# Product-key stage: maxima subtracted as the bias of per-head exponentials, one list in PSUM, the next tile normalised by ScalarE

## Chip, core and metric

The kernel runs on one core of a Trainium2 chip. It computes a whole decoder of four layers in one launch. The metric is device time in microseconds, the median of three runs. The engines are TensorE (PE; PEld is its weight load), VectorE (DVE), ScalarE (ACT), GpSimd (POOL) and SyncE (SP), each with its own instruction queue; they are kept in order by semaphores.

## The reference, cut to the stage

The input is 8 x 128 x 256: eight tiles of 128 tokens with 256 features. Twelve blocks follow one another; the change lies in the ninth, the feed-forward of the third layer, a retrieval by product keys:

```python
x = x + _L2_ffn_ref(_layernorm(x, axis=-1), ...)

h = silu(x W_up + b_up) W_down + b_down          # 256 -> 1024 -> 128
q = (h W_q), 2 halves x 8 heads x 64
sim = einsum('pbthn,hkpn->pbthk', q, keys)       # 2 x 8 heads x 45 similarities
scores, idx = lax.top_k(sim, 8)
all_scores = scores[0][..., :, None] + scores[1][..., None, :]
sc, pk = lax.top_k(all_scores, 8)                # the best 8 of 64 pairs
z = einsum('btd,bthkd->bthk', h, down_embed[indices])
z = silu(z * softmax(sc))
out = einsum('bthk,bthkd->btd', z, up_embed[indices])
```

The kernel gathers nothing. For each head it forms all 45 x 45 = 2025 pair weights as the outer product of the exponentials of the two halves, masks those below the eighth best pair, and multiplies with z for all 2025 entries.

## The kernel before

The stage handles one tile of 128 tokens after the other, n = 0 to 7. A tile has 16 items g = 16n + s: eight heads for entries 0 to 1023 (s = 0 to 7), and eight heads for entries 1024 to 2024 (s = 8 to 15). The order of every engine is written out by hand in loops over n and s; the preparation of tile n+1, and the normalising of tile n+2, are placed between items of tile n.

For one item, GpSimd makes the outer product of 23 x 45 weights (`L2f_outer`, L1320) into a ring of seven buffers `P_r`, running up to five items ahead. VectorE compares it with the threshold and multiplies by z, the mask (`L2f_mask`, L3132). The product of mask and weights is taken by VectorE (`L2f_prod`, L3140), or by GpSimd for s = 2, 5, 10 and 13 (`L2f_poolprod`, L1328), into a ring of six buffers `Q_r`. ScalarE applies silu with the reciprocal of the sum as its scale (`L2f_silu`, L1988). TensorE transposes and sums over heads in PSUM (`L2f_acc`, L4347). After eight items ScalarE copies the sums out (`L2f_gt`, L1992 to L1997), and TensorE multiplies by the up embedding (`L2f_out`, L4356); VectorE adds the residual (`L2f_resid`, L3144). z itself is a product of TensorE in PSUM (`L2f_z`, L4337), one for each half of a tile; TensorE issues z of half 0 of tile n+1 at s = 15, behind the transposes of item 13 (`L2f_acc(g - 2)`), and the mask of s = 0 waits for it.

Preparation of tile n+1 on the way through tile n: up projection (L4158) at s = 0, its silu (`L2f_he`, L1862) at s = 2, down, query and similarity products (L4165, L4171, L4284) at s = 3 to 5 with the evictions L1946, L1950 and L1954 (`L2f_simc`) on ScalarE. All of these use `pro`, two PSUM banks. Then:

- `L2f_top` (VectorE, s = 7): 16 MAX8 instructions (L3096) into `top8`, and a subtraction of the maximum from the lists into `top8s` (L3099).
- `L2f_sub` (GpSimd, s = 7): the maximum is subtracted from all 720 similarities (L1307). It is queued ahead of the outer product of item 12.
- `L2f_exp` (ScalarE, s = 10, behind silu 9): a table load (L1957), the exponential of the lists (L1959), and that of the 720 similarities (L1961).
- `L2f_rstd` (ScalarE, s = 10, for tile n+2): a table load (L1847), Ln (L1849), Exp (L1851). The next silu loads its table again.
- `L2f_u` (VectorE, s = 13, for tile n+2): the normalised tile (L2981). TensorE transposes it at s = 14 (`L2f_uT`, L4149), behind the transposes of item 12, and ScalarE copies it at s = 15 (`L2f_unT`, L1857).
- `L2f_thresh` (VectorE, s = 15): the 64 candidate products of each head (L3104), the eighth best (L3107), the sum of the best eight (L3110) and its reciprocal (L3112).
- GpSimd's first outer product of tile n+1 is queued at s = 11 of tile n, behind the outer product of item 15, and waits for L1961. Its product of item 13 is queued two outer products later.

## Time and profile before

| | |
|---|---|
| median of 3 runs | 2097.64 us (2092.2 to 2108.24) |
| the profiled execution's own time | 2106.74 us |
| its span | 2105.0 us, mean granted TensorE clock 0.942 |
| busy over the span | PE 88%, PEld 65%, DVE 70%, ACT 51%, POOL 52% |
| outer product on GpSimd (L1320) | 128 x, mean 1969 ns |
| product on GpSimd (L1328) | 32 x, mean 2153 ns |
| product on VectorE (L3140), 1024 elements, one input in PSUM | 96 x, mean 1212 ns |
| Ln over one column with a pointer bias (L1849), Exp over one column (L1851) | mean 296 and 203 ns |
| GpSimd's subtraction (L1307) waiting for the maxima (L3096) | 9.3 us in 5 of 8 |

The profile is that of one execution. Busy times count an engine's instructions; idle time before an instruction is put down to the instruction whose semaphore came last. In the timeline, instructions of one line that follow one another are merged into one row with their count, so that a row's duration runs from the first start to the last end. Line numbers are those of the kernel before.

### The profile page before, as it was taken

The page shows a single profiled execution, that of the slowest core. Times are in us where ns is not written, and L with a number is a line of the kernel's source. Part 1 is how long each engine was busy: PE and PEld are TensorE (multiplying, and loading weights), DVE is VectorE, ACT ScalarE, POOL GpSimd, SP SyncE. Part 2 cuts the span into 40 slices and gives each one's busy share as a digit, 9 for nine tenths or more (in the row PEclk, how much of TensorE's full clock was granted, in tenths as well). Part 3 has the DMA queues.
Part 4 walks back from the last instruction along what each step waited for, and adds up shares of the span by engine and source line. Part 5 has one row for each costly group of instructions (what it writes and reads, how often), then busy time and mean ns, then how long its engine had stood idle before and what let it go on. Part 6 is the DMA issues. An engine that isn't in the chain of part 4 may idle for free.

```text
span 2105.0 us, 31292 instructions
## 1 busy us (share of the span) xinstructions
PE 1847.7 (88%) x11466; PEld 1373.4 (65%) x11466; DVE 1483.6 (70%) x2496; ACT 1071.2 (51%) x2328; POOL 1095.8 (52%) x800
## 2 busy tenths in 40 slices
PE   7767789799899987899999999968888789998999
PEld 5111148545789975677777777757777665567887
DVE  5788943465764576677777777589999978866554
ACT  4444421244322254666666666556667556655443
POOL 3699930121691064655555555499999940023321
PEclk9788989689899998999999999989999989999999
DMA  5211001040400000110000000000000001000000
GB/s 165 46 35 35 0 1 59 20 161 0 181 1 1 1 21 21 51 34 1 1 1 1 1 1 31 28 3 1 1 1 1 26 26 58 1 1 1 6 9 9
DMA packets 20544, 54.87 MB, mean 26 GB/s; under 512 B 8111, under 2 KB 11864, under 8 KB 17960
## 3 DMA queue, kind: packets, MB, share of 16 engines
q1 hardware_dynamic: 20392, 52.88, 7.5%
q8 instruction: 92, 1.51, 0.3%
q14 instruction: 60, 0.49, 0.1%
HBM read 44.48 MB, written 1.05 MB: 22 GB/s over the span
## 4 chain that ended last, share of the span: by engine, by line
PE 54%; DVE 19%; POOL 11%; issue 8%; ACT 7%; SPq 1%; DMA 0%; DVEq 0%; POOLq 0%; ACTq 0%
POOL sbuf L1320 5%; PE psum L4187 4%; DVE sbuf L2319 4%; PE psum L4250 3%; PE psum L3537 2%; POOL sbuf L1328 2%; PE psum L4347 1%; DVE psum L3132 1%; PE psum L4653 1%; PE psum L4219 1%; PE psum L4235 1%; PE psum L4191 1%; PE psum L4199 1%; PE psum L3516 1%; ACT sbuf L1902 1%
## 5 line engine op out<-in xcount | busy, mean ns | idle before, releaser
L1320 POOL TENSOR_TENSOR sbuf<-sbuf 128x1035 f32<-128x1035 f32 x128 | 248.3, 1969 | 0.9 <-ACT sbuf L1961 0.9
L4347 PE MATMUL psum<-sbuf 128*128 128x128 f32 (+1 forms) x1024 | 146.6, 294 | 57.3 <-ACT sbuf L1988 41.7
L1988 ACT ACTIVATE sbuf<-sbuf 128x1001 f32<-128x1001 f32 (+1 forms) x128 | 141.9, 1139 | 97.4 <-DVE sbuf L3140 64.6
L4347 PEld LDWEIGHTS psum<-sbuf 128*128 128x128 f32 (+1 forms) x1024 | 127.9, 154 | 78.1 <-ACT sbuf L1988 58.6
L1275 POOL TENSOR_TENSOR sbuf<-sbuf 128x512 f32<-128x512 f32 x64 | 66.7, 1042 | 187.7 <-DVE sbuf L3004 187.7
L1115 POOL TENSOR_TENSOR sbuf<-sbuf 128x1024 f32<-128x1024 f32 x64 | 150.0, 2355 | 17.2 <-DVE sbuf L2319 16.1
L2319 DVE TENSOR_TENSOR_SCAN sbuf<-psum,sbuf 128x1024 f32<-128x1024 f32 x64 | 144.6, 2277 | 14.4 <-POOL sbuf L1115 7.5
L1902 ACT ACTIVATE sbuf<-psum,sbuf 128x128 f32<-128x128 f32 x256 | 90.4, 365 | 107.2 <-DVE sbuf L2998 107.2
L3483 PE MATMUL psum<-sbuf 96*128 96x512 bf16 x256 | 82.8, 432 | 61.7 <-DVE sbuf L2319 35.4
L3132 DVE SCALAR_TENSOR_TENSOR psum<-sbuf,psum 128x1024 f32<-128x1024 f32 (+1 forms) x96 | 122.3, 1274 | 11.5 <-PE psum L4337 4.2
L1445 ACT ACTIVATE psum<-psum,sbuf 128x1016 f32<-128x1016 f32 x64 | 68.9, 1081 | 120.9 <-PE psum L3483 120.9
L4187 PE MATMUL psum<-sbuf 128*128 128x512 f32 x256 | 123.9, 607 | 3.5 <-POOL sbuf L1271 3.5
L3140 DVE TENSOR_TENSOR sbuf<-psum,sbuf 128x1024 f32<-128x1024 f32 (+1 forms) x96 | 116.4, 1212 | 3.3
L3483 PEld LDWEIGHTS psum<-sbuf 96*128 96x128 bf16 x256 | 18.5, 102 | 139.0 <-DVE sbuf L2319 67.1
L4250 PE MATMUL psum<-sbuf 128*128 128x256 bf16 x768 | 94.6, 273 | 14.4 <-POOL sbuf L1283 14.2
L1281 POOL TENSOR_TENSOR sbuf<-sbuf 128x512 f32<-128x512 bf16 x64 | 74.4, 1163 | 49.7 <-DVE sbuf L3017 48.0
L4250 PEld LDWEIGHTS psum<-sbuf 128*128 128x128 bf16 x768 | 71.3, 98 | 39.8 <-POOL sbuf L1283 30.7
L1373 POOL TENSOR_TENSOR sbuf<-sbuf 128x1024 f32<-128x1024 f32 x16 | 30.8, 1944 | 121.8 <-DVE sbuf L3333 121.8
L2993 DVE TENSOR_TENSOR sbuf<-psum,sbuf 128x512 f32<-128x512 f32 x64 | 44.3, 691 | 57.1 <-ACT sbuf L1886 57.1
L1283 POOL TENSOR_TENSOR sbuf<-sbuf 128x512 bf16<-128x512 f32 x64 | 81.1, 1268 | 5.0
L3516 PE MATMUL psum<-sbuf 128*32 128x512 f32 x256 | 78.9, 748 | 3.9 <-POOL sbuf L1115 3.8
L1328 POOL TENSOR_TENSOR sbuf<-sbuf 128x1024 f32<-128x1024 f32 (+1 forms) x32 | 68.9, 2153 | 18.3 <-DVE sbuf L3132 18.3
(811 smaller groups left out, 5093.2 us busy)
## 6 DMA issues: line engine op xcount, KB each, us to landing
sbuf<-sbuf SPq DMA_DIRECT2D x50, 128.0 KB, 2.4
sbuf<-w_p_d SPq DMA_DIRECT2D x8, 512.0 KB, 3.9
sbuf<-w_qkv_d SPq DMA_DIRECT2D x3, 768.0 KB, 4.2
sbuf<-w_e_d SPq DMA_DIRECT2D x1, 2048.0 KB, 8.0
sbuf<-w_gu_d SPq DMA_DIRECT2D x1, 2048.0 KB, 10.2
sbuf<-w_gu_d SPq DMA_DIRECT2D x2, 1024.0 KB, 8.0
sbuf<-w_dn_d SPq DMA_DIRECT2D x1, 2048.0 KB, 16.5
sbuf<-w_q_d SPq DMA_DIRECT2D x1, 2048.0 KB, 8.5
```

Source lines behind the costliest of these rows:

```text
L1115: pool.tensor_tensor(L0a_hc[i % 4][:, :], L0a_hs[i % 2][:, :], L0a_Cr[g % 4][:, :], ALU.mult).then_inc(hc_done, 1)
L1320: pool.tensor_tensor(P_r[g % 7][:, :, :], rows.unsqueeze(2).to_broadcast([128, 23, 45]), cols.unsqueeze(1).to_broadcast([128, 23, 45]), AL ...
L1328: pool.tensor_tensor(Q_r[g % 6][:, 0:w], M_r[L2f_pool_items(g) % 2][:, 0:w], Pf_r[g % 7][:, o:o + w], ALU.mult).then_inc(poolprod_done, 1)
L1902: last = act.activation(prob[:, h, :], L2x_s[:, h, :], ACT.Exp, bias=smax[:, h:h + 1], accum_out=esum[:, h:h + 1])
L1988: act.activation(Q_r[g % 6][:, 0:w], Q_r[g % 6][:, 0:w], ACT.Silu, scale=q8_p[n % 2][:, h:h + 1]).then_inc(silu_done, 1)
L2319: dve.tensor_tensor_scan(L0a_hs[i % 2][:, :], L0a_dAf[i % 2][:, :], L0a_us[i % 3][:, :], 0.0, ALU.mult, ALU.add).then_inc(scan_done, 1)
L3132: dve.scalar_tensor_tensor(M[:, 0:w], Pf_r[g % 7][:, o:o + w], t8_p[n % 2][:, h, 7:8], zps[:, 0:w], ALU.is_ge, ALU.mult).then_inc(mask_don ...
L3140: dve.tensor_tensor(Q_r[g % 6][:, 0:w], Mps[:, 0:w], Pf_r[g % 7][:, o:o + w], ALU.mult).then_inc(prod_done, 1)
L3483: last = pe.matmul(out[:, 512 * h:512 * h + 512], rows, L0a_stack[g % 4][0:96, a, 512 * h:512 * h + 512], start=True, stop=True)
L4187: last = pe.matmul(L2x_q[:, :, :], xs[:, vq, c, :], wq[:, c, 512 * g:512 * g + 512], start=c == 0, stop=c == 1)
L4250: last = pe.matmul(L2x_out[:, :], cat16[:, h, :], w_p3[p][:, 4 * (i % 8) + h, :], start=i % 8 == 0 and h == 0 and p == 0, stop=i % 8 == 7 ...
L4347: last = pe.matmul(Gps[0:m, c, :], Q_r[g % 6][:, 128 * c:128 * c + m], ident[:, :], start=h == 0 and c % 4 == 0, stop=h == 7, skip_group_c ...
```

## The change

The subtraction of the maxima goes from GpSimd and VectorE to ScalarE. The lists of the eight largest lie beside the similarities, in columns 45 to 52 of rows that are now 53 long. VectorE's second instruction in `L2f_top` only negates the 16 maxima. `L2f_exp` is 24 activations, each with the negated maximum of its head as a pointer bias: eight over 53 columns for the second half (similarities and list together), eight over 8 columns for the first half's list, written to PSUM (`top8e`, in a gap of `pro`), and eight over 45 columns. `L2f_u` for tiles 2 to 7 becomes `L2f_standard` on ScalarE, three activations that wait on one another, at s = 12, between silu 11 and silu 12. TensorE gets two waits, and its transposed tile moves to other columns of `pro`.

```diff
--- before.py
+++ after.py
@@ -568,18 +568,18 @@
         GT = view(sbuf, 35862, [16, 128])
         he = view(sbuf, 38934, [8, 128])
         qc = view(sbuf, 39958, [8, 128])
-        sim_p = [view(sbuf, 40982 + 720 * p, [2, 8, 45]) for p in range(2)]
-        top8 = view(sbuf, 42422, [2, 8, 8])
+        sim_p = [view(sbuf, 40982 + 848 * p, [2, 8, 53]) for p in range(2)]
+        top8n = view(sbuf, 42678, [2, 8])
         h2T_p = [view(sbuf, 46152 + 128 * p, [128]) for p in range(2)]
         cand = view(sbuf, 46408, [8, 8, 8])
         t8_p = [view(sbuf, 46920 + 64 * p, [8, 8]) for p in range(2)]
         q8_p = [view(sbuf, 47048 + 8 * p, [8]) for p in range(2)]
         d8 = view(sbuf, 47064, [8])
-        top8s = view(sbuf, 47072, [2, 8, 8])
         zps = view(psum, 3072, [1024])
         Mps = view(psum, 1024, [1024])
         Gps = view(psum, 2048, [8, 128])
         pro = view(psum, 0, [1024])
+        top8e = view(psum, 360, [8, 8])
 
         L2f_pool_heads = (2, 5)
 
@@ -697,17 +697,17 @@
                      'clip': 2, 'expo': 4, 'magic': 4, 'sum': 8, 'q': 1, 'k': 8, 'v': 12, 'sq': 12, 'ss': 4, 'lnvar': 13, 'rstd': 13, 'norm': 20,
                      'vc': 12, 'qTc': 9, 'kTc': 12, 'score': 12, 'max': 24, 'exp': 24, 'recip': 12, 'prob': 4, 'pT': 24, 'pTc': 24, 'o': 12,
                      'cat': 7, 'proj': 20, 'resid': 28, 'hi': 5, 'mid': 5, 'lo': 5}
-        L2f_start = {'stats': 46, 'ln': 16, 'factor': 15, 'u': 30, 'uT': 18, 'unT': 18, 'up': 12, 'down': 4, 'q': 65, 'score': 76, 'max': 88,
+        L2f_start = {'stats': 46, 'ln': 16, 'factor': 15, 'u': 30, 'centred': 13, 'prep': 11, 'uT': 18, 'unT': 18, 'up': 12, 'down': 4, 'q': 65, 'score': 76, 'max': 88,
                      'sub': 24, 'exp': 88, 'mask': 1, 'prod': 40, 'silu': 16, 'sum': 40, 'proj': 84, 'resid': 36}
         L3a_start = {'const': 9, 'bn': 46, 'stats': 62, 'u': 38, 'uT': 26, 'unT': 26, 'q': 73, 'v': 76, 'lnvar': 77, 'rstd': 77, 'norm': 84,
                      'vc': 76, 'qTc': 73, 'kTc': 76, 'score': 84, 'max': 96, 'exp': 96, 'recip': 76, 'pT': 88, 'pTc': 88, 'o': 76, 'cat': 71,
-                     'proj': 92, 'resid': 44, 'sub': 32, 'aoT': 4, 'bias': 4}
-        L3x_start = {'context': 1, 'clip': 34, 'expo': 36, 'k': 72, 'vc': 84, 'summary': 1, 'spread': 8, 'gate': 12, 'oclip': 64, 'prep': 11,
+                     'proj': 92, 'resid': 44, 'sub': 24, 'aoT': 4, 'bias': 4}
+        L3x_start = {'context': 1, 'clip': 34, 'expo': 36, 'k': 72, 'vc': 84, 'summary': 1, 'spread': 8, 'gate': 12, 'oclip': 64, 'prep': 17,
                      'oexpo': 64, 'exp': 128, 'qT': 64, 'ln': 24, 'osum': 64, 'oq': 16, 'ratio': 36, 'sum': 168, 'factor': 23, 'norm': 100,
                      'proj': 100, 'resid': 52}
         L3f_start = {'const': 10, 'bn': 54, 'stats': 70, 'u': 46, 'uT': 34, 'unT': 34, 'q': 81, 'v': 84, 'ss': 68, 'lnvar': 85, 'rstd': 85, 'vc': 92,
                      'qTc': 81, 'kTc': 84, 'score': 116, 'mask': 129, 'max': 128, 'exp': 136, 'recip': 92, 'prob': 68, 'pT': 120, 'pTc': 120,
-                     'o': 92, 'cat': 79, 'proj': 108, 'resid': 60, 'sub': 64, 'ur': 8, 'xr': 16, 'mod': 4, 'low': 4, 't': 4, 'gate': 20, 'up': 20,
+                     'o': 92, 'cat': 79, 'proj': 108, 'resid': 60, 'sub': 56, 'ur': 8, 'xr': 16, 'mod': 4, 'low': 4, 't': 4, 'gate': 20, 'up': 20,
                      'silu': 144, 'prod': 136}
         L0a_later_loaded = stack.enter_context(nc.semaphore('L0a_later_loaded'))
         L0a_stack_loaded = [stack.enter_context(nc.semaphore(f'L0a_stack{s}_loaded')) for s in range(4)]
@@ -1301,11 +1301,6 @@
 
             pool.wait_ge(resid_done, L2x_start['resid'] + 8)
 
-            def L2f_sub(n):
-                pool.wait_ge(simc_done, n + 1)
-                pool.wait_ge(max_done, L2f_start['max'] + n + 1)
-                pool.tensor_tensor(sim_p[n % 2][:, :, :, :], sim_p[n % 2][:, :, :, :], top8[:, :, :, 0:1].to_broadcast([128, 2, 8, 45]), ALU.subtract).then_inc(sub_done, 1)
-
             def L2f_outer(g):
                 n, half, h = g // 16, g // 8 % 2, g % 8
                 if g % 16 == 0:
@@ -1316,7 +1311,7 @@
                     else:
                         pool.wait_ge(prod_done, L2f_start['prod'] + L2f_dve_items(g - 6))
                 rows = sim_p[n % 2][:, 0, h, 22 * half:22 * half + 23]
-                cols = sim_p[n % 2][:, 1, h, :]
+                cols = sim_p[n % 2][:, 1, h, 0:45]
                 pool.tensor_tensor(P_r[g % 7][:, :, :], rows.unsqueeze(2).to_broadcast([128, 23, 45]), cols.unsqueeze(1).to_broadcast([128, 23, 45]), ALU.mult).then_inc(outer_done, 1)
 
             def L2f_poolprod(g):
@@ -1327,14 +1322,11 @@
                     pool.wait_ge(sum_done, L2f_start['sum'] + g - 5)
                 pool.tensor_tensor(Q_r[g % 6][:, 0:w], M_r[L2f_pool_items(g) % 2][:, 0:w], Pf_r[g % 7][:, o:o + w], ALU.mult).then_inc(poolprod_done, 1)
 
-            L2f_sub(0)
             for g in range(5):
                 L2f_outer(g)
             for n in range(8):
                 for s in range(16):
                     g = 16 * n + s
-                    if s == 7 and n < 7:
-                        L2f_sub(n + 1)
                     if L2f_by_pool(g):
                         L2f_poolprod(g)
                     if g + 5 < 128:
@@ -1850,11 +1842,21 @@
                 act.wait_ge(ln_done, L2f_start['ln'] + n + 1)
                 act.activation(st0[:, 9:10], st0[:, 8:9], ACT.Exp, scale=-0.5).then_inc(factor_done, 1)
 
+            def L2f_standard(n):
+                act.wait_ge(stats_done, L2f_start['stats'] + 2 * n + 2)
+                act.activation(st0[:, 10:11], st0[:, 6:7], ACT.Copy, scale=-1.0).then_inc(prep_done, 1)
+                act.wait_ge(uT_done, L2f_start['uT'] + n)
+                act.wait_ge(prep_done, L2f_start['prep'] + n - 1)
+                act.activation(u0[:, :], x[:, n, :], ACT.Identity, bias=st0[:, 10:11]).then_inc(centred_done, 1)
+                act.wait_ge(centred_done, L2f_start['centred'] + n - 1)
+                act.wait_ge(factor_done, L2f_start['factor'] + n + 1)
+                act.activation(u0[:, :], u0[:, :], ACT.Copy, scale=st0[:, 9:10]).then_inc(u_done, 1)
+
             def L2f_unT(n):
                 act.wait_ge(uT_done, L2f_start['uT'] + n + 1)
                 if n == 0:
                     act.wait_ge(ratio_done, L2x_start['ratio'] + 32)
-                act.activation(unT0[:, 0:2, :], L2x_uT[:, :, :] if n == 0 else pro[:, 0:256].rearrange('p (c s) -> p c s', c=2), ACT.Copy).then_inc(unT_done, 1)
+                act.activation(unT0[:, 0:2, :], L2x_uT[:, :, :] if n == 0 else pro[:, 768:1024].rearrange('p (c s) -> p c s', c=2), ACT.Copy).then_inc(unT_done, 1)
 
             def L2f_he(n, a, b):
                 act.wait_ge(up_done, L2f_start['up'] + n + 1)
@@ -1951,14 +1953,19 @@
 
             def L2f_simc(n):
                 act.wait_ge(score_done, L2f_start['score'] + n + 1)
-                act.activation(sim_p[n % 2][:, :, :, :], pro.rearrange('p (q c) -> p q c', q=2)[:, :, 0:360].rearrange('p q (h k) -> p q h k', h=8), ACT.Copy).then_inc(simc_done, 1)
+                act.activation(sim_p[n % 2][:, :, :, 0:45], pro.rearrange('p (q c) -> p q c', q=2)[:, :, 0:360].rearrange('p q (h k) -> p q h k', h=8), ACT.Copy).then_inc(simc_done, 1)
 
             def L2f_exp(n):
                 act.preload_act_table_set('natural_log_exp_and_others')
                 act.wait_ge(shift_done, n + 1)
-                act.activation(top8s[:, :, :, :], top8s[:, :, :, :], ACT.Exp).then_inc(exp_done, 1)
-                act.wait_ge(sub_done, L2f_start['sub'] + n + 1)
-                act.activation(sim_p[n % 2][:, :, :, :], sim_p[n % 2][:, :, :, :], ACT.Exp).then_inc(simexp_done, 1)
+                for h in range(8):
+                    act.activation(sim_p[n % 2][:, 1, h, :], sim_p[n % 2][:, 1, h, :], ACT.Exp, bias=top8n[:, 1, h:h + 1])
+                for h in range(8):
+                    last = act.activation(top8e[:, h, :], sim_p[n % 2][:, 0, h, 45:53], ACT.Exp, bias=top8n[:, 0, h:h + 1])
+                last.then_inc(exp_done, 1)
+                for h in range(8):
+                    last = act.activation(sim_p[n % 2][:, 0, h, 0:45], sim_p[n % 2][:, 0, h, 0:45], ACT.Exp, bias=top8n[:, 0, h:h + 1])
+                last.then_inc(simexp_done, 1)
 
             def L3a_rstd(n):
                 act.wait_ge(stats_done, L3a_start['stats'] + n + 1)
@@ -2031,6 +2038,8 @@
                             L2f_exp(n + 1)
                             if n < 6:
                                 L2f_rstd(n + 2)
+                        if s == 12 and n < 6:
+                            L2f_standard(n + 2)
                         if s == 15 and n < 6:
                             L2f_unT(n + 2)
             L2f_silu(127)
@@ -3090,18 +3099,18 @@
                 dve.wait_ge(simc_done, n + 1)
                 if n > 0:
                     dve.wait_ge(cand_done, n)
-                    dve.wait_ge(sub_done, L2f_start['sub'] + n)
+                    dve.wait_ge(simexp_done, n)
                 for p in range(2):
                     for h in range(8):
-                        last = dve.max(top8[:, p, h, :], sim_p[n % 2][:, p, h, :])
+                        last = dve.max(sim_p[n % 2][:, p, h, 45:53], sim_p[n % 2][:, p, h, 0:45])
                 last.then_inc(max_done, 1)
                 dve.wait_ge(max_done, L2f_start['max'] + n + 1)
-                dve.tensor_tensor(top8s[:, :, :, :], top8[:, :, :, :], top8[:, :, :, 0:1].to_broadcast([128, 2, 8, 8]), ALU.subtract).then_inc(shift_done, 1)
+                dve.tensor_scalar(top8n[:, :, :], sim_p[n % 2][:, :, :, 45], -1.0, None, ALU.mult).then_inc(shift_done, 1)
 
             def L2f_thresh(n):
                 t8, q8 = t8_p[n % 2], q8_p[n % 2]
                 dve.wait_ge(exp_done, L2f_start['exp'] + n + 1)
-                dve.tensor_tensor(cand[:, :, :, :], top8s[:, 0, :, :].unsqueeze(3).to_broadcast([128, 8, 8, 8]), top8s[:, 1, :, :].unsqueeze(2).to_broadcast([128, 8, 8, 8]), ALU.mult).then_inc(cand_done, 1)
+                dve.tensor_tensor(cand[:, :, :, :], top8e[:, :, :].unsqueeze(3).to_broadcast([128, 8, 8, 8]), sim_p[n % 2][:, 1, :, 45:53].unsqueeze(2).to_broadcast([128, 8, 8, 8]), ALU.mult).then_inc(cand_done, 1)
                 dve.wait_ge(cand_done, n + 1)
                 for h in range(8):
                     last = dve.max(t8[:, h, :], cand[:, h, :, :])
@@ -3172,8 +3181,6 @@
                             L2f_stats(n + 2)
                         if s == 7:
                             L2f_top(n + 1)
-                        if s == 13 and n < 6:
-                            L2f_u(n + 2)
                         if s == 15:
                             L2f_thresh(n + 1)
             L3a_values(0)
@@ -4145,12 +4152,16 @@
 
             def L2f_uT(n):
                 pe.wait_ge(u_done, L2f_start['u'] + n + 1)
+                if n > 2:
+                    pe.wait_ge(resid_done, L2f_start['resid'] + n - 2)
                 for k in range(2):
-                    last = pe.transpose(L2x_uT[:, k, :] if n == 0 else pro[:, 128 * k:128 * k + 128], u0[:, 128 * k:128 * k + 128], ident[:, :])
+                    last = pe.transpose(L2x_uT[:, k, :] if n == 0 else pro[:, 768 + 128 * k:896 + 128 * k], u0[:, 128 * k:128 * k + 128], ident[:, :])
                 last.then_inc(uT_done, 1)
 
             def L2f_up(n, a, b):
                 pe.wait_ge(unT_done, L2f_start['unT'] + n + 1)
+                if n > 0:
+                    pe.wait_ge(cand_done, n)
                 if n > 2:
                     pe.wait_ge(resid_done, L2f_start['resid'] + n - 2)
                 for j in range(a, b):
```

## Rows read from the trace of the kernel before

**Rows 1.** Busy us (instructions) of PE, PEld, DVE, ACT, POOL in one tile; clock, DMA, GB/s

```profile
1459.00:1502.00 43.00, 37.25 (x255) 32.38 (x254) 41.10 (x62) 29.87 (x42) 42.18 (x22) 0.95 0.00 1
```

**Rows 2.** Timeline, end of tile 2: start us, us, engine, line, tiles, count [idle before <-releaser]

```profile
1490.95 1.28 ACT L1957 ACT_TABLE_LOAD   x1
...
1492.24 0.31 ACT L1959 ACTIVATE sbuf<-sbuf 128x128 f32<-128x128 f32 x1
...
1492.46 0.79 ACT L1961 ACTIVATE sbuf<-sbuf 128x720 f32<-128x720 f32 x1
...
1493.27 1.28 ACT L1847 ACT_TABLE_LOAD   x1
...
1496.40 3.17 ACT L1988 ACTIVATE sbuf<-sbuf 128x1001 f32<-128x1001 f32 x3
...
1497.59 4.29 PE L4347 MATMUL psum<-sbuf 128*128 128x128 f32 x24 [2.60 <-ACT sbuf L1988]
...
1501.72 0.38 PE L4149 MATMUL psum<-sbuf 128*128 128x128 f32 x2
...
1502.81 1.89 PE L4337 MATMUL psum<-sbuf 128*128 128x512 f32 x4
...
1504.82 1.29 DVE L3132 SCALAR_TENSOR_TENSOR psum<-sbuf,psum 128x1024 f32<-128x1024 f32 x1 [0.20 <-POOL sbuf L1320]
```

**Rows 3.** Waits of the stage: engine, line, releaser: us in total, times, longest us

```profile
DVE psum L3132 <- PE psum L4337: 4.2, 4, 2.8
```

**Rows 4.** Source lines of four operations: duration ns min/median/max, first to last start, forms

```profile
L2981 DVE TENSOR_SCALAR sbuf<-sbuf x8: 402/500/1827, 1297.7 to 1624.2; 128x256 f32<-128x256 f32 x8
...
L3104 DVE TENSOR_TENSOR sbuf<-sbuf x8: 1240/1522/1880, 1368.1 to 1672.2; 128x512 f32<-128x512 f32 x8
...
L1320 POOL TENSOR_TENSOR sbuf<-sbuf x128: 1916/1951/2386, 1369.9 to 1708.2; 128x1035 f32<-128x1035 f32 x128
...
L4337 PE MATMUL psum<-sbuf x64: 571/592/1062, 1364.5 to 1699.0; 128*128 128x512 f32 x48, 128*128 128x489 f32 x16
```

**Rows 5.** Timeline of ACT, two pairs of activations with a pointer operand

```profile
436.92 0.51 ACT L1605 ACTIVATE sbuf<-sbuf 128x256 f32<-128x256 f32 x1 [5.50 <-DVE sbuf L2567]
437.33 0.49 ACT L1606 ACTIVATE sbuf<-sbuf 128x256 f32<-128x256 f32 x1
...
564.12 0.28 ACT L1714 ACTIVATE sbuf<-sbuf 128x1 f32<-128x1 f32 x1
564.31 0.28 ACT L1715 ACTIVATE sbuf<-sbuf 128x1 f32<-128x1 f32 x1
```

**Rows 6.** Timeline, tiles 0, 5 and 6: table load ahead of exponentials, mask 0 behind it

```profile
1404.84 1.28 ACT L1957 ACT_TABLE_LOAD   x1
...
1420.74 1.29 DVE L3132 SCALAR_TENSOR_TENSOR psum<-sbuf,psum 128x1024 f32<-128x1024 f32 x1 [0.20 <-POOL sbuf L1320]
...
1618.77 1.28 ACT L1957 ACT_TABLE_LOAD   x1
...
1633.86 1.29 DVE L3132 SCALAR_TENSOR_TENSOR psum<-sbuf,psum 128x1024 f32<-128x1024 f32 x1 [0.20 <-POOL sbuf L1320]
...
1661.73 1.28 ACT L1957 ACT_TABLE_LOAD   x1
...
1675.88 1.29 DVE L3132 SCALAR_TENSOR_TENSOR psum<-sbuf,psum 128x1024 f32<-128x1024 f32 x1 [0.20 <-POOL sbuf L1320]
```

**Rows 7.** Timeline, start of the stage

```profile
1367.80 0.31 ACT L1959 ACTIVATE sbuf<-sbuf 128x128 f32<-128x128 f32 x1 [1.00 <-DVE sbuf L3099]
...
1369.94 13.37 POOL L1320 TENSOR_TENSOR sbuf<-sbuf 128x1035 f32<-128x1035 f32 x7 [0.91 <-ACT sbuf L1961]
```

**Rows 8.** Timeline, tile 0: GpSimd and VectorE around the normalising pass

```profile
1406.85 5.73 POOL L1320 TENSOR_TENSOR sbuf<-sbuf 128x1035 f32<-128x1035 f32 x3
...
1410.91 1.83 DVE L2981 TENSOR_SCALAR sbuf<-sbuf 128x256 f32<-128x256 f32 x1
```

**Rows 9.** Busy us and granted clock just after TensorE restarts, tile 2

```profile
1499.00:1500.00 1.00, 1.00 (x7) 1.00 (x6) 0.90 (x2) 0.57 (x1) 1.00 (x1) 0.50 0.00 0
```


## The prediction

> **What bounds the kernel now.** The change touches one stage, 1365 to 1720 us. I read first the busy times by window: in a whole tile (43 us) VectorE is busy for 41.10 us and GpSimd for 42.18, TensorE for 37.25 and ScalarE for 29.87 [rows 1]. So the first reading is that VectorE and GpSimd share the bound and ScalarE has a third of its time free. Busy time does not say when that free time lies, so I read next the timeline around the end of one tile, item 9 of tile n to item 0 of tile n+1 [rows 2]. ScalarE there loads the table set at 1490.95, runs its two exponentials (1492.24 to 1493.27), loads twice more around the rstd pair, and runs silu 10 to 12 from 1496.40 to 1499.57. TensorE, idle for 2.60 us waiting for silu 10, then does transposes 10 to 12, the transpose of the next normalised tile (1501.72), transposes 13, and only then the matmuls of z for the next tile (1502.81, 1.89 long, so until 1504.70). VectorE's mask 0 of the next tile waits for z and starts at 1504.82. The two are 0.12 us apart: in this stretch the chain ScalarE, TensorE, z has next to no slack. The waits confirm it: mask was already held by z four times, 4.2 us in total, 2.8 at most [rows 3]. Whatever is put on ScalarE between silu 9 and silu 13 therefore comes out as VectorE time. This is where the sum is made.
>
> **What leaves VectorE and GpSimd.** GpSimd loses its subtraction (1.45 us, eight times). VectorE loses the normalising pass for six tiles, median 0.50 us but up to 1.83 [rows 4], and its candidate product, 1.52 us at the median for 512 elements with both inputs in SBUF, gets one input from PSUM; the stage's own product does 1024 elements with one input in PSUM in 1.2 us (table of the profile), so 512 take at most that and at least half of it; I take 0.7, saving 0.8. That is about 1.7 us of VectorE and 1.45 of GpSimd per tile. If these engines kept the bound, 42.5 us a tile would become about 41, or 10 to 12 us over the stage. I cost all this at nothing, because VectorE spends it waiting for z: both removed items lie behind item 9.
>
> **What comes onto ScalarE: the exponentials.** 24 activations replace two. Durations overlap, so starts must be used. With a per-partition pointer operand, two activations of one column start 0.19 us apart, two of 256 columns 0.41 apart [rows 5]; this is 0.187 + 0.00087 per column. 53, 8 and 45 columns then take 0.23, 0.19 and 0.23: 8 x 0.65 = 5.2 us, against 1.03 now (1492.24 to 1493.27). Lower end: without the pointer 128 columns take 0.22 from start to start [rows 2], 0.11 + 0.00087 per column, so 8 x 0.42 = 3.4 us. Upper end: no overlap at all, 24 x 0.30 (the Ln over one column, table) = 7.2. I take 5.2, since the rows with a pointer are the same form. Added: 4.2 us.
>
> **The normalising pass.** It comes behind silu 11 and ahead of silu 12: a copy of one column (0.20, as the rstd's Exp in the table), an Identity over 256 columns with a pointer (0.51), a scaled copy (0.49, both [rows 5]), each waiting on the one before, so without overlap: 1.2 us (0.9 to 1.5). No table load comes with it: the Identity and Copy evictions between silus have none today.
>
> **Sum for one tile.** Silu 12 ends at 1499.57 + 4.17 + 1.2 = 1504.9. Transposes 12 start 0.1 later, the normalised tile's transpose 0.87 after that (1505.9), z ends 2.98 behind it (1501.72 to 1504.70 in the rows) and mask 0 starts at 1509.0, that is 18.05 us after the table load. Now the six tiles that also normalise take 15.9, 14.5, 13.9, 15.3, 14.2 and 15.1 from that load to mask 0 (88.9 in all; [rows 6] has the first and the last of the six). 6 x 18.05 - 88.9 = 19.4 us. The work from mask 0 to the next load, 28 us (the five periods from 1420.74 to 1633.86 are 42.6 each, less the mean of 14.6 from load to mask), hangs on the same z and does not shrink: of what the change removes nothing lies there but GpSimd's subtraction, and GpSimd stands behind VectorE's mask 2 there.
>
> **Tile 6** has no normalising pass and no rstd, but GpSimd's first outer product of tile 7 waits for the last exponential, and its product 13 is queued behind it. From the load: 1.29 + 5.2 + 0.1, two outer products at 1.95 [rows 4], product 13 at 2.15 (table; 12.7), silu 13 (1.07), transposes and z (3.0): 16.8 against 14.15 now [rows 6]: 2.6 us. In the other six tiles product 13 is ready at 12.7 too, 1.3 ahead of where silu 13 can start.
>
> **The start.** The exponentials of tile 0 have no other work beside them. Now the small exponential starts at 1367.80 and GpSimd's first outer product at 1369.94 [rows 7]; then 1367.80 + 5.2 + 0.1 = 1373.1. 3.2 us, kept because tile 0 runs behind GpSimd's first seven outer products.
>
> **The lock.** The two-input subtraction over the lists becomes a tensor_scalar over 16 elements. The trace: the removed normalising pass is also a tensor_scalar in SBUF, and it needs 0.40 us alone but 1.83 when it starts at 1410.91 in a run of outer products that ends at 1412.58, and it ends just behind them [rows 4, 8]. So the new 16-element instruction can wait up to 1.95 us for the outer product in flight; today GpSimd mostly is between two instructions there, waiting for the maxima (9.3 us in five of the eight, table). Bounds: nothing, or 1.8 in each of seven tiles (12.6). By where GpSimd's outer products end today against VectorE's list subtraction, four of seven tiles would be caught (1.3 to 1.8 us), three not. Most of it is free: in tiles 1 to 5 the chain enters ScalarE through silu 9, which starts 1 us after its product is there, behind two copies of sums that hang on TensorE. I estimate that 0.7, 0.7, 0.2 and 0.2 remain, 1.8 us.
> The Trainium skill says it as a rule (SBUF - State Buffer, Who interferes with whom): a VectorE instruction in a two-port mode and a GpSimd instruction exclude each other for the whole instruction. By that rule, the trace agrees, 1.43 of the 1.83 us are a wait, and it is the new instruction that would meet it in every tile: rival D.
>
> **The clock.** TensorE's idle time ahead of transposes 10 grows from 2.6 to 6.8 us. After the present gap the granted clock was 0.50 (1.2 GHz) [rows 9], and the 24 matmuls took 4.29 us. The new transposes 12 start 3.2 us behind the restart (1501.8 to 1505.0), and today the transpose behind them, 4.1 us after the restart, runs at full speed (0.38 for two). I take 0.3 us a tile, 1.8; bounds 0 and (transposes 12, 13 and z, 4 us, at half clock) 24.
>
> **New waits of no cost.** Up-projection behind the candidate product: TensorE comes to it behind z, the product ends 4 us before. The transpose behind an earlier residual: that was added at item 12 of a tile, the transpose stands at item 14. The maxima behind the previous exponentials: those ended a tile ago.
>
> **Sum.** 19.4 + 2.6 + 3.2 + 1.8 + 1.8 = 28.8, so 29 us. The profiled execution took 2106.74 us (span 2105.0) and would become 2136; it lies 9 us over the median of the three runs, 2097.64, which becomes 2127 (+1.4%). Measurement of this kernel tells about 1% from no change.
>
> **Rivals.**
> A: ScalarE is not what holds mask 0 (not slower). Place: the 24 exponentials and the pass, between silu 9 and silu 12. They would have to cost together less than 3.1 us (14.8 average now - 11.65 for the rest of the chain) for VectorE and GpSimd to keep the bound; then their 1.45 to 1.7 us a tile count. For: ScalarE is 70% busy and both others over 95%. Against: even the lower end, 3.4 + 0.9, is above it. Price: 2097.6 - 11 = 2087. Chance 0.07.
> B: exponentials overlap more than the pointer rows say (3.4 us). 8 x 1.8 less: 2127 - 14 = 2113, within 1%. For: nothing depends on the one in front. Against: rows 5. Chance 0.12.
> C: the clock stays low until z is done. z alone costs 1.9 more in six tiles, 11 us: 2138. For: the longest z matmul of the trace is 1.06 us against 0.59 [rows 4]. Against: the clock had come back by transposes 12. Chance 0.12.
> D: the lock is hit in every tile and is not hidden, 1.8 x 7 instead of 1.8: 2138. Chance 0.09.
> E: the normalising pass does not run where it stands (a table load comes with it, 1.28 in six tiles): 2135. Chance 0.03.
> My forecast: 0.57.
>
> **Range and chances.** 2111 to 2142 takes in B, C, D and E and leaves out A and the far ends of the clock. Slower by over 1% (above 2118.6): forecast, C, D, E, 0.81. Within 1%: B and half of A, 0.15. Faster by over 1%: 0.04, since even A's full price is 0.5%.
>
> **What would show it.** From the table load of L2f_exp to mask 0 of the next tile about 18 us in tiles 0 to 5; mask waiting for z (TensorE) in each, 2.5 to 5 us, some 25 in all; the 24 exponentials 5.2 us from first to last start; GpSimd's busy share down from 97% to under 90% in the stage, with idle time released by ScalarE; the new tensor_scalar between 0.1 and 2 us in two clusters; a tile of 46 us instead of 42.5. Wrong would be: mask 0 released by the reciprocal as today; exponentials under 0.15 us apart; or a mask 0 that starts with z done long before, in which case rival A holds.

## The result, and the profile after

The changed kernel takes 2140.57 us (median of 4; 2126.8 to 2150.1) against 2096.6 beside it, ratio 1.0181 [1.0146, 1.0216]. The forecast was 2127, range 2111 to 2142, slower. The profiled execution took 2140.63 us, span 2138.7, 33.7 us more than before. The stages ahead of this one ended 6.9 us earlier in it (first MAX8 at 1358.69, before 1365.63; both stand at the same place in the code), so the stage itself gave away about 40 us. Those 6.9 us are not put down to the change: in the kernels below, which do not touch those stages, the first MAX8 starts anywhere from 1351.8 to 1367.7. The stage is therefore compared from trace to trace by its own length, from the first to the last mask 0: 304.0 us before, 340.4 after.

Lines moved: the table load L1957 is L1959, the exponentials are L1962, L1964 and L1967, the pass L1847, L1850 and L1853, MAX8 L3105, the negation L3108, mask L3141, product on VectorE L3149, candidates L3113, silu L1995, transposes and sums L4358, z L4348, outer product L1315. In some of the experiments they differ again by a few lines.

One whole tile by busy time (columns as in [rows 1]), the page's groups of mask and outer product, and the waits of VectorE in the stage:

```profile
1472.15:1520.16 48.01, 37.45 (x253) 33.05 (x251) 40.90 (x60) 34.43 (x65) 39.56 (x21) 0.89 0.00 1
```
```profile
L1315 POOL TENSOR_TENSOR sbuf<-sbuf 128x1035 f32<-128x1035 f32 x128 | 245.1, 1947 | 32.4 <-ACT sbuf L1967 32.4
...
L3141 DVE SCALAR_TENSOR_TENSOR psum<-sbuf,psum 128x1024 f32<-128x1024 f32 (+1 forms) x96 | 122.2, 1273 | 48.9 <-PE psum L4348 42.4
```
```profile
DVE psum L3141 <- PE psum L4348: 42.4, 9, 6.7
DVE sbuf L3105 <- ACT sbuf L1956: 7.0, 4, 5.6
```

Tiles 1 to 5 take 47.6 to 48.0 us instead of 42.0 to 43.5 (47.7 and 42.6 on average). GpSimd, 98% busy before, is busy for 39.56 of 48.01; ScalarE went from 29.87 to 34.43 and is still the least busy of the four. The mask's wait for z, 4.2 us in [rows 3], is 42.4. The chain behind it is seen in the timeline of the end of tile 2, the counterpart of [rows 2]:

```profile
1500.93 1.28 ACT L1959 ACT_TABLE_LOAD   x1
1502.23 1.95 ACT L1962 ACTIVATE sbuf<-sbuf 128x53 f32<-128x53 f32 x8
...
1504.08 1.59 ACT L1964 ACTIVATE psum<-sbuf 128x8 f32<-128x8 f32 x8
...
1505.61 1.88 ACT L1967 ACTIVATE sbuf<-sbuf 128x45 f32<-128x45 f32 x8
...
1507.51 1.28 ACT L1839 ACT_TABLE_LOAD   x1
...
1510.64 2.15 ACT L1995 ACTIVATE sbuf<-sbuf 128x1001 f32<-128x1001 f32 x2
...
1511.83 5.38 PE L4358 MATMUL psum<-sbuf 128*128 128x128 f32 x24 [7.41 <-ACT sbuf L1995]
1512.35 0.68 DVE L3113 TENSOR_TENSOR sbuf<-psum,sbuf 128x512 f32<-128x512 f32 x1
1512.70 0.18 ACT L1847 ACTIVATE sbuf<-sbuf 128x1 f32<-128x1 f32 x1
1512.98 0.51 ACT L1850 ACTIVATE sbuf<-sbuf 128x256 f32<-128x256 f32 x1
...
1513.52 0.51 ACT L1853 ACTIVATE sbuf<-sbuf 128x256 f32<-128x256 f32 x1
1513.94 3.16 ACT L1995 ACTIVATE sbuf<-sbuf 128x1001 f32<-128x1001 f32 x3
...
1517.01 0.47 PE L4158 MATMUL psum<-sbuf 128*128 128x128 f32 x2
...
1518.18 1.88 PE L4348 MATMUL psum<-sbuf 128*128 128x512 f32 x4
...
1520.16 1.29 DVE L3141 SCALAR_TENSOR_TENSOR psum<-sbuf,psum 128x1024 f32<-128x1024 f32 x1 [5.49 <-PE psum L4348]
```

From table load to mask 0 it is 19.23 us, 13.87 before. Split it where TensorE restarts: load to restart 10.90 (before 6.64), restart to the transposed tile 5.18 (before 4.13), from there to mask 0 3.15 (before 3.10). The first part grew by the exponentials. The second part grew because the clock is low for longer: granted clock by the microsecond, from the same tile:

```profile
1507.00:1508.00 1.00, 0.00 (x0) 0.00 (x0) 1.00 (x2) 0.98 (x4) 0.43 (x1) 0.50 0.00 0
...
1512.00:1513.00 1.00, 1.00 (x6) 1.00 (x7) 1.00 (x2) 0.91 (x3) 1.00 (x1) 0.50 0.06 16
...
1516.00:1517.00 1.00, 1.00 (x6) 1.00 (x5) 0.00 (x0) 1.00 (x2) 1.00 (x1) 0.50 0.00 0
1517.00:1518.00 1.00, 1.00 (x10) 1.00 (x10) 0.00 (x0) 0.58 (x3) 1.00 (x2) 0.92 0.00 0
```

and from the kernel before, behind its restart at 1497.59:

```profile
1500.00:1501.00 1.00, 1.00 (x8) 1.00 (x8) 0.97 (x2) 0.46 (x1) 1.00 (x2) 0.70 0.00 0
1501.00:1502.00 1.00, 1.00 (x12) 1.00 (x10) 1.00 (x2) 1.00 (x2) 1.00 (x1) 1.00 0.00 0
```

TensorE stood still for 7.41 us, was granted half of its 2.4 GHz from 1506.9 on, 4.9 us ahead of its restart, and got the rest back at 1517.2, 5.3 us behind it. Before, the clock fell at 1497.2, 0.4 us ahead of the restart, and was back at 1500.6, 3.0 us behind it. The 24 transposes took 5.38 us, before 4.29 [rows 2]; in a kernel below, at full clock, 8 take 1.04 to 1.10. In each of tiles 1 to 5 of the changed kernel the clock is low for 10.2 us; in the kernel before there are five low stretches of 3.4 us in these five tiles, and none in tile 3.

The lock, in the timeline of tile 0 (counterpart of [rows 8]) and as a source line:

```profile
1389.41 9.56 POOL L1315 TENSOR_TENSOR sbuf<-sbuf 128x1035 f32<-128x1035 f32 x5
...
1392.01 1.81 DVE L3105 MAX8 sbuf<-sbuf 128x8 f32<-128x45 f32 x16 [5.58 <-ACT sbuf L1956]
1393.85 5.14 DVE L3108 TENSOR_SCALAR sbuf<-sbuf 128x16 f32<-128x16 f32 x1
```
```profile
L3108 DVE TENSOR_SCALAR sbuf<-sbuf x8: 175/1744/5143, 1360.5 to 1683.4; 128x16 f32<-128x16 f32 x8
```

Sixteen elements take 0.175 us alone (tile 0's own maxima, at 1360.5) and 5.14 us when five outer products follow one another on GpSimd. The instruction began during the third of the five, which ended at 1395.1, and ended behind the fifth (1398.97). In five of the other six tiles it took 1.7 to 2.0 us: three times it ended with the outer product that was running when it began, twice with the next one, and each time another outer product followed at once. In the sixth it took 0.18. What decides how many go first was not tested.

### The profile page after: what moved, and what is told of

It is laid out like the page before. It is cut to its first block, busy times and chain, and to the rows that moved or that the text cites. A ratio compares the mean times of both kernels' runs of the same rounds, so it can differ in the third digit from the quotient of the medians.

```text
span 2138.7 us, 31477 instructions
## 1 busy us (share of the span) xinstructions
PE 1849.9 (86%) x11466; PEld 1382.7 (65%) x11466; DVE 1483.8 (69%) x2490; ACT 1112.6 (52%) x2522; POOL 1081.9 (51%) x792
## 3 DMA queue, kind: packets, MB, share of 16 engines
HBM read 44.48 MB, written 1.05 MB: 21 GB/s over the span
## 4 chain that ended last, share of the span: by engine, by line
PE 56%; DVE 18%; ACT 11%; POOL 7%; issue 7%; SPq 1%; DMA 0%; DVEq 0%; POOLq 0%; ACTq 0%
PE psum L4198 4%; PE psum L4358 3%; DVE sbuf L2328 3%; PE psum L4261 3%; PE psum L3544 2%; PE psum L4664 1%; PE psum L4230 1%; PE psum L4246 1%; POOL sbuf L1115 1%; PE psum L4202 1%; PE psum L4418 1%; ACT sbuf L1995 1%; POOL sbuf L1315 1%; PE psum L4210 1%; ACT sbuf L1904 1%
## 5 line engine op out<-in xcount | busy, mean ns | idle before, releaser
L1315 POOL TENSOR_TENSOR sbuf<-sbuf 128x1035 f32<-128x1035 f32 x128 | 245.1, 1947 | 32.4 <-ACT sbuf L1967 32.4
L4358 PE MATMUL psum<-sbuf 128*128 128x128 f32 (+1 forms) x1024 | 155.2, 308 | 85.4 <-ACT sbuf L1995 66.3
L4358 PEld LDWEIGHTS psum<-sbuf 128*128 128x128 f32 (+1 forms) x1024 | 138.5, 163 | 104.0 <-ACT sbuf L1995 83.6
L1995 ACT ACTIVATE sbuf<-sbuf 128x1001 f32<-128x1001 f32 (+1 forms) x128 | 141.9, 1141 | 94.1 <-DVE sbuf L3149 71.4
L3141 DVE SCALAR_TENSOR_TENSOR psum<-sbuf,psum 128x1024 f32<-128x1024 f32 (+1 forms) x96 | 122.2, 1273 | 48.9 <-PE psum L4348 42.4
L3149 DVE TENSOR_TENSOR sbuf<-psum,sbuf 128x1024 f32<-128x1024 f32 (+1 forms) x96 | 116.4, 1212 | 3.3
```

What stands on the lines that cost most here:

```text
L1315: pool.tensor_tensor(P_r[g % 7][:, :, :], rows.unsqueeze(2).to_broadcast([128, 23, 45]), cols.unsqueeze(1).to_broadcast([128, 23, 45]), AL ...
L1995: act.activation(Q_r[g % 6][:, 0:w], Q_r[g % 6][:, 0:w], ACT.Silu, scale=q8_p[n % 2][:, h:h + 1]).then_inc(silu_done, 1)
L3141: dve.scalar_tensor_tensor(M[:, 0:w], Pf_r[g % 7][:, o:o + w], t8_p[n % 2][:, h, 7:8], zps[:, 0:w], ALU.is_ge, ALU.mult).then_inc(mask_don ...
L3149: dve.tensor_tensor(Q_r[g % 6][:, 0:w], Mps[:, 0:w], Pf_r[g % 7][:, o:o + w], ALU.mult).then_inc(prod_done, 1)
L4358: last = pe.matmul(Gps[0:m, c, :], Q_r[g % 6][:, 128 * c:128 * c + m], ident[:, :], start=h == 0 and c % 4 == 0, stop=h == 7, skip_group_c ...
```

## The experiments

Two theories ran against each other. The first is the prediction's: ScalarE's longer queue makes z late, and z makes mask 0 late. The second came up on the way: the delay sits ahead of everything that TensorE does at a tile's end, the preparation of the next tile included, so that z's place does not matter. A smaller question was what the lock costs.

**The pass back on VectorE** (changed kernel otherwise).

```diff
...
-                        if s == 12 and n < 6:
-                            L2f_standard(n + 2)      # ScalarE
...
+                        if s == 13 and n < 6:
+                            L2f_u(n + 2)             # VectorE
```


> The changed kernel with the normalising pass back on VectorE (item 13). Theory (what ScalarE runs between silu 9 and silu 13 comes out one for one behind z): the pass's 1.2 us leave six tiles, so the table load to mask 0 of the next tile falls from 19.4 to about 18.2 us, or to 17.8 if TensorE's transposes 12 and 13 no longer have a transpose between them; 7 to 9 us under the changed kernel, about 35 over the one before. Rival (the exponentials alone hurt because of the lock at the new tensor_scalar): also about 35 over before, but then the distance from load to mask 0 stays at 19.4.

2142.97 us, ratio 1.0187 [1.0153, 1.0222]: nothing gained. The distance from load to mask 0 stayed at 19.2 to 19.5 us. That is what the rival expected, but for another reason: the kernel without the lock, below, keeps 19.35 to 19.5 us in tiles 3 to 5. The timeline of tile 2 in this kernel shows why the pass bought nothing.

```profile
1516.29 0.20 ACT L1843 ACTIVATE sbuf<-sbuf 128x1 f32<-128x1 f32 x1
...
1516.53 2.18 DVE L2978 TENSOR_SCALAR sbuf<-sbuf 128x256 f32<-128x256 f32 x1 [1.95 <-ACT sbuf L1843]
1517.81 5.21 ACT L1985 ACTIVATE sbuf<-sbuf 128x1001 f32<-128x1001 f32 x5
...
1518.99 5.38 PE L4348 MATMUL psum<-sbuf 128*128 128x128 f32 x24 [7.40 <-ACT sbuf L1985]
...
1527.33 1.29 DVE L3129 SCALAR_TENSOR_TENSOR psum<-sbuf,psum 128x1024 f32<-128x1024 f32 x1 [1.37 <-PE psum L4338]
```

Silu 10 to 14 now run without a gap, and the transposes still take 5.38 us, and mask 0 comes 8.34 us after the restart, as with the pass (8.33). So the pass's 1.2 us on ScalarE lay beside transposes that the low clock had stretched. VectorE in its turn stands 1.95 us for the reciprocal root, which waits behind the exponentials, and then takes 2.18 for a pass of 0.40 (the lock).

**The pass alone** (kernel before, with the pass on ScalarE).

```diff
...
+                        if s == 12 and n < 6:
+                            L2f_standard(n + 2)      # ScalarE
...
-                        if s == 13 and n < 6:
-                            L2f_u(n + 2)             # VectorE
```


> The kernel before with the normalising pass alone moved to ScalarE, item 12; exponentials, lists and subtraction as before. Theory: the chain silu 11, pass, silu 12, silu 13, z grows by 1.2 us in six tiles with next to no slack, minus nothing: 5 to 8 us over the kernel before, z releasing mask 0. Rival (VectorE holds mask 0, the chain has slack): VectorE loses 0.4 to 1.8 us a tile, so 3 to 6 us faster than before.

2099.62, ratio 0.999 [0.997, 1.001]. 1.2 us more on ScalarE, for 0.4 to 1.8 less on VectorE, cost nothing here: the 5 to 8 us of loss that the theory expected are outside the interval. The rival's gain of 3 to 6 us is inside it, and in the two traces the stage is 3.3 us shorter (300.7 for 304.0), 1.75 of it in tile 0. With the run above: the pass is not in the loss; the rest of the change, the 24 exponentials with the lists and the negation, carries it. What the negation adds by the lock is priced below.

**z early** (changed kernel).

```diff
                     g = 16 * n + s
+                    if s == 12 and n < 7:
+                        L2f_z(n + 1, 0)
                     if g >= 2:
                         L2f_acc(g - 2)
...
-                        if s == 15:
-                            L2f_z(n + 1, 0)
```


> The changed kernel, with TensorE's z of the next tile (half 0) put ahead of transposes 10 in its queue instead of behind transposes 13; nothing else. Theory (mask 0 is late only because z stands behind work that waits for ScalarE): mask 0 is released by the threshold instead, about 5 us earlier in tiles 0 to 5; about 1 us of each comes back because the up projection is no longer done earlier relative to mask 0; 20 to 30 us under the changed kernel. Rival (ScalarE's added work or GpSimd's wait for the exponentials is itself the bound of a tile): within 8 us of the changed kernel.

2139.73, ratio 1.0178 [1.0149, 1.0207]. The expectation was wrong, and partly through a slip: z writes the PSUM that mask 15 of the tile still reads. Waits of TensorE and VectorE in this kernel:

```profile
PE psum L4348 <- DVE psum L3141: 49.4, 7, 8.0
...
DVE sbuf L3105 <- ACT sbuf L1956: 28.0, 7, 5.8
...
DVE psum L3141 <- PE psum L4348: 4.1, 8, 2.1
```

The mask waits no more (4.1 us), but TensorE stands for mask 15 instead (49.4), and the MAX8 group waits for the similarities (28.0, in the changed kernel 7.0). So this run alone does not separate the theories. On the kernel before, the same edit was tried as well:

> The kernel before, with z of the next tile ahead of transposes 10 in TensorE's queue. The mask's 4.2 us of waiting for z would go, and TensorE would use 1.9 of its 2.6 idle us for z. If z is on the path of the kernel before (my reading of its timeline): 0.5 to 1 us per tile, 4 to 7 us in all, ratio 0.997. If VectorE and GpSimd bound it (41.1 and 42.2 us busy of 43): no change, ratio 1.000.

2134.96, ratio 1.0139 [1.011, 1.0167]: 29 us lost by moving the two matmul calls of z forward, where a small gain or none was expected. The timeline of a tile's end in it:

```profile
1504.05 1.04 PE L4347 MATMUL psum<-sbuf 128*128 128x128 f32 x8
1512.17 3.78 PE L4337 MATMUL psum<-sbuf 128*128 128x512 f32 x4 [7.08 <-DVE psum L3132]
```

z, at the lower clock (0.50 until 1517.6), takes 3.78 us, twice its 1.89 in [rows 2], and the transposes are queued behind it. No added ScalarE work is in this kernel, and tiles 1 to 5 take 47.7 us on average all the same (mask 0 from 1420.73 to 1659.25). So a pause of some 7 us of TensorE at a tile's end can come from another wait and give a tile as long.

**z in the middle** (changed kernel), the same test without that wait: in front of transposes 12, where mask 15 is long done.

```diff
+                    if s == 14 and n < 7:
+                        L2f_z(n + 1, 0)
                     if g >= 2:
                         L2f_acc(g - 2)
...
-                        if s == 15:
-                            L2f_z(n + 1, 0)
```


> The changed kernel with z of the next tile one group of transposes and the next tile's transposes ahead of its place: in front of transposes 12 instead of behind transposes 13. There mask 15, whose PSUM z overwrites, has ended long ago (in the changed kernel mask 15 ends at 1511.2 and transposes 12 start at about 1516.2), so z waits for nothing, unlike in the kernels with z in front of transposes 10, in which TensorE stood 7 us per tile in front of z. If the late z is what the added ScalarE work costs: mask 0 some 2.5 to 3 us earlier in seven tiles, 18 to 20 us, ratio 1.009. If the preparation of the next tile through TensorE (transposes, up projection, copy of the similarities, maxima, exponentials), which hangs on the same queue and does not move, closes the same loop: the MAX8 group waits for the similarities instead, 0 to 1 us per tile, ratio 1.015 to 1.018.

2145.61, ratio 1.0211 [1.0183, 1.0239]. Tiles 47.6 to 47.8 us, as in the changed kernel. Its timeline and waits:

```profile
1520.08 3.68 PE L4358 MATMUL psum<-sbuf 128*128 128x128 f32 x16 [6.86 <-ACT sbuf L1995]
1523.55 3.06 PE L4348 MATMUL psum<-sbuf 128*128 128x512 f32 x4
...
1526.70 1.29 DVE L3141 SCALAR_TENSOR_TENSOR psum<-sbuf,psum 128x1024 f32<-128x1024 f32 x1 [4.78 <-PE psum L4348]
```
```profile
DVE sbuf L3105 <- ACT sbuf L1956: 17.3, 7, 5.4
```

Mask 0 comes 6.6 us after the restart instead of 8.3, so the edit did what it says; the tile kept its length, and the MAX8 group waits 17.3 us instead of 7.0. In tiles 1 to 5 that wait is 1.9 us each, and it is what mask 0 had gained: from the load to mask 0 it is 17.4 to 17.6 us instead of 19.2 to 19.5, from mask 0 to the next load 30.2 instead of 28.2 to 28.8. That is the second theory: the preparation (transposes, up projection, similarities, maxima, exponentials) closes a loop over the same late restart, as long as the loop over z. "Mask 0 is held by z" is true and not the whole bound.

**No lock** (changed kernel).

```diff
-                dve.tensor_scalar(top8n[:, :, :], sim_p[n % 2][:, :, :, 45], -1.0, None, ALU.mult).then_inc(shift_done, 1)
+                dve.tensor_reduce(top8n[:, :, :], sim_p[n % 2][:, :, :, 45:46], AX.X, ALU.max, negate=True).then_inc(shift_done, 1)
```


> The changed kernel, with the negated maxima made by a negating tensor_reduce instead of a tensor_scalar (same 16 values). Theory (the tensor_scalar waits for the shared port): its row falls from 1.7 to 5.1 us to about 0.2 in all tiles. Tile 0 gains 4 us, the others 0.5 each since silu 9 had slack: 5 to 8 us under the changed kernel. Rival (the long rows are the instruction itself): its duration stays or the time doesn't move.

2132.65, ratio 1.0159 [1.0129, 1.0189], and all eight take 0.18 us:

```profile
L3108 DVE TENSOR_REDUCE sbuf<-sbuf x8: 181/182/185, 1357.3 to 1673.2; 128x16 f32<-128x16 f32 x8
```

From the first to the last mask 0 of the stage it is 333.2 us instead of 340.4. Of these 7.2 us, 5.6 are tile 0 (50.8 for 56.4); the other six share 1.6. The intervals of the two ratios overlap, so the price of the lock rests on this comparison of two traces.

**Both, z early and no lock.**

> The changed kernel with both edits of before at once: z of the next tile ahead of transposes 10 in TensorE's queue, and the maxima negated by a tensor_reduce instead of a tensor_scalar. With z early alone the tile kept its 47.8 us: the wait for z (5 us) went, and in its place stood 3.6 us of the MAX8 group waiting for the copy of the similarities and 3.4 to 4.9 us of the tensor_scalar behind outer products. Theory 1 (the two waits in its place are one behind the other, and the lock is the larger, since GpSimd runs five outer products without a pause there): without the lock 3 us in each of seven tiles go, tile 44.7 us, in all 20 us under z early alone and 12 under no lock alone: ratio to the kernel before about 1.008. Theory 2 (the tile is a loop through ScalarE, exponentials, silus, transposes, up projection, copy of the similarities, maxima, exponentials, and every wait off it only fills what is free): the lock lies in that loop too, but VectorE then waits for silu's buffers and the transposes instead; no more than tile 0's 5 us: ratio 1.015.

2125.23, ratio 1.0103 [1.0079, 1.0126], tiles 45.0 to 46.3, between the two expectations: with z early the MAX8 group is late, and a lock of 3.7 us (median with z early alone) behind it does stand on the path. Without the second table load as well:

> As z_early_no_lock, and the table load ahead of the rstd pair inside the loop is left out (the set is already there, loaded 6.5 us earlier for the exponentials): 1.28 us less on ScalarE between silu 9 and silu 10, in six tiles. Theory 2 (ScalarE's queue sets the tile): 1.28 x 6 = 7.7 us less than z_early_no_lock, ratio lower by 0.0037. Theory 1 (VectorE and GpSimd have the bound again once both waits are gone): no difference between the two.

2122.86, ratio 1.0082 [1.0053, 1.0111], and the same tiles to 0.1 us. The load taken out bought nothing there: TensorE stood for mask 15 at a tile's end (40.0 us in both), not for ScalarE. The kernel before with z early and one load gave 1.0139 [1.0113, 1.0164], again nothing on top of z early, and neither of its two expectations was met:

> The kernel before, z early as in before_z_early, and without the second load of the same table set ahead of the rstd pair inside the loop, 1.28 us of ScalarE in six tiles. If ScalarE between silu 9 and silu 12 is on the path: up to 7 us less than before_z_early, ratio 0.993 to 0.995. If VectorE and GpSimd bound the kernel before: no change, ratio 1.000 for both.

**One load** (changed kernel), the cleanest measure of what a microsecond of ScalarE's queue is worth. The second load of the same table set, ahead of the rstd pair, is left out inside the loop.

```diff
-                if n > 1:
-                    act.preload_act_table_set('natural_log_exp_and_others')
```


> The changed kernel without the second load of the same table set, ahead of the rstd pair inside the loop: 1.28 us less on ScalarE between silu 9 and silu 10, in six tiles, and nothing else. If ScalarE's queue behind silu 9 sets the tile, each us on it is a us of the tile: 7.7 us less than the changed kernel, ratio to the kernel before 1.0145, tiles 1 to 5 at 46.4 us instead of 47.7. Rival (the tile follows GpSimd and VectorE, and ScalarE's time is only seen in it): ratio 1.018, unchanged.

2125.76, ratio 1.0126 [1.0094, 1.0159]. The stage is 12.6 us shorter in the trace (327.8 for 340.4), where 7.7 were expected. Tiles 1 to 5 average 45.7 us (from 1419.09 to 1647.73) against 47.7: 2.0 us for 1.28. The pauses and transposes of tiles 1 and 2 in it:

```profile
1456.78 4.37 PE L4356 MATMUL psum<-sbuf 128*128 128x128 f32 x24 [5.44 <-ACT sbuf L1993]
...
1502.47 5.24 PE L4356 MATMUL psum<-sbuf 128*128 128x128 f32 x24 [5.99 <-ACT sbuf L1993]
```

Behind the shorter pause (5.44) the transposes take 4.37 us, and that tile is 45.1 long; behind 5.99 they take 5.24, and it is 46.4. In these two the clock came back earlier in the shorter tile (2.9 us behind the restart against 5.0), and the transposes account for 0.9 of the 1.3 us between them. The length of the pause alone does not decide it: in tile 0 of this kernel 24 transposes took 4.63 us behind 7.47, and in tile 0 of the last kernel below 5.36 behind 3.30.

**Three edits together** (changed kernel, z in the middle, no lock, one load).

> The three edits together on the changed kernel: z in front of transposes 12, the maxima negated by a tensor_reduce, one table load instead of two. If each works on the path by itself: 18 + 5 + 7.7 = 31 us less than the changed kernel, ratio 1.003 to 1.005. If the loop through the preparation binds: 7.7 + 5 + a part of 2 us per tile as in z_early_no_lock, about 15 to 25 us, ratio 1.006 to 1.011.

2124.42, ratio 1.0106 [1.0073, 1.0139]. From first to last mask 0 it is 321.5 us against 327.8 with one load alone: the difference is tile 0 and the lock, z's place adds nothing. The second expectation, by the loop through the preparation, held.

**The pass on ScalarE, one load** (kernel before), the try at a faster one.

> The kernel before with the normalising pass of the next tile on ScalarE (1.2 us there, 0.4 to 1.8 us less on VectorE), which alone changed nothing (0.999), and the second table load of the rstd pair left out (1.28 us less on ScalarE, same place). ScalarE's queue behind silu 9 is then as long as in the kernel before, and VectorE has 0.4 us less, 1.8 in tile 0. If ScalarE's queue and VectorE bound the tile together: 1.28 of z's lateness goes, 0.4 to 1.2 us per tile, 3 to 7 us, ratio 0.996 to 0.998, faster than both kernels. If GpSimd (42.2 of 43 us) is the bound: 0.999 as with the pass alone.

2094.92, ratio 0.9987 [0.9962, 1.0011]: no difference that can be told. Its tile 2:

```profile
1451.29:1493.35 42.06, 35.63 (x253) 30.48 (x251) 40.17 (x60) 28.71 (x42) 41.23 (x22) 1.00 0.00 1
```

The granted clock is 1.00 over the whole tile (0.96 before, over the tile from mask 0 to mask 0), the transposes run at full speed (8 in 1.04 to 1.10 us), and tiles 1 to 6 average 42.3 us against 42.5. They average 42.3 with the pass alone too, so the 1.28 us taken off ScalarE's queue between these two kernels gave nothing. GpSimd is busy for 41.23 of 42.06. This fits a kernel before in which GpSimd and VectorE bound the tile about as closely as the chain does: 1.2 us added to the chain or 1.28 taken off it change nothing, 4.2 cost all of it and the clock. The load left out of the kernel before by itself was not run.

## Why the prediction was right, and where it was off

Right in sign and near in size. 2140.6 against 2127 is 13.5 us, 1.4 us inside the upper end of the range, and the four executions lie between 2126.8 and 2150.1, so some luck is in that. The loss was forecast at 28.8 us; the ratio makes it 38, the traces 39.6 in the stage. The mechanism held (ScalarE's queue delays TensorE's restart, and z then holds mask 0). Two terms were mis-sized: the clock, and the lock. Step by step:

- *The exponentials.* 5.2 us forecast, 5.26 measured (1502.23 to 1507.49); the restart of TensorE came 4.26 us later from the load, against 4.2 added. The spacing from the pointer rows [rows 5] held for 53, 8 and 45 columns, into PSUM too. Rival B falls.
- *The pass.* 1.2 us on ScalarE, as forecast, but not on the path: taking it off the changed kernel gave nothing, and putting it on the kernel before cost nothing. So "whatever is put on ScalarE between silu 9 and silu 13 comes out as VectorE time" was wrong for it. This did not spoil the sum, by luck: in [rows 2] silu 12 ends at 1499.57 and transposes 12 begin at about 1500.85, a slack of 1.3 us that the pass just fills. The exponentials alone give the same figure, 13.87 + 4.17 = 18.04 us. Rival E falls, no load came with it.
- *The clock.* Here the sum was too small: 0.3 us a tile, where 1.0 to 1.3 were needed. The transposes 10 to 12 lasted 5.38 us, and the next tile's transposes ended up 16.1 us after the load where 14.95 was forecast. The argument had been that the clock, seen at full speed 4.1 us behind the restart before (it was back after 3.0), would be back for transposes 12. Behind a pause of 7.4 instead of 2.6 us it came back 5.3 us behind the restart, and transposes 12, from 1515.3 to the transposed tile at 1517.0, ran at half of it. Rival C had the mechanism half right: the transposes paid, z did not (1.88 us).
- *Load to mask 0.* 18.35 with the clock term, measured 19.2 to 19.5 in tiles 0 to 5 (116.4 in sum against 88.9): 27.5 us, forecast 21.2. Tile 6: 16.88, forecast 16.8; there product 13 ended 12.75 us behind the load, forecast 12.7. Start: from MAX8 to mask 0 3.1 us more, forecast 3.2.
- *The lock.* The term "four of seven caught, 1.8 us remain" was mis-sized: 7.2 us by the kernel without it. Six of seven were caught. Its upper bound for one wait, one outer product in flight, failed in tile 0: it lasted over the rest of three, 5.14 us. Rival D (a lock in every tile, 1.8 each) had the count nearly right and the place wrong: most of the price is tile 0, the other six share 1.6 us. By the Trainium skill (SBUF - State Buffer, Who interferes with whom) a VectorE instruction in a two-port mode and a GpSimd instruction exclude each other, each for the whole instruction. The rows of tile 0 show more than that, a wait across GpSimd instructions that follow each other.
- *Mask 0 to the next load* did not shrink, as forecast; it grew by 2.05 us in the other six tiles together and by 4.15 in tile 0. The 4.15 are the lock: without it this distance is 32.6 us in tile 0, before 32.9. TensorE's two new waits cost nothing, as forecast: neither line is among its waits.
- *Hidden gains.* The candidate product fell to 0.68 us (forecast 0.7), GpSimd's subtraction went, and neither bought anything.

The parts add up: 3.15 (start) + 27.5 + 2.7 (tile 6) + 2.05 + 4.15 = 39.55 us, less the 6.9 from ahead of the stage, and 1.05 us behind it: 33.7 of span. Of the 10.7 us by which the stage exceeds the forecast 28.8, 6.3 are load to mask 0, the clock above all, and 4.4 are mask 0 to the next load, mostly the lock of tile 0.

Rival A's point, that a chain with enough slack would leave VectorE and GpSimd the bound, was not this change's case. The two kernels with the pass on ScalarE suggest that it is the case of the kernel before: its stage became 3.3 us shorter when VectorE lost the pass. It was not tested by an edit to GpSimd.

What stays open: the tiles 1 to 5 of most of the kernels fall near four lengths (42 to 43, 45.1, 46.4 and 47.7 us), whatever was edited. Their mean clocks are mostly 0.96 to 1.00 in the first and 0.89 to 0.93 in the last, but why they fall on steps was not tested. Nor was the part of the 24 exponentials' loss that is the clock measured by itself. One observation bears on the steps: in the changed kernel the low stretches of the clock in tiles 1 to 5 begin 47.8 us apart, which is the length of a tile.
